# Routing begun two steps earlier, row scatters around GpSimd's products, one group less at the end

## The chip, the cores and the metric

The kernel runs on one core of one Trainium2 chip. The metric is the device time of one launch in microseconds (us), lower is better. A core has five engines that run side by side and wait for each other through semaphores: TensorE (PE in the rows, its weight loads PEld), VectorE (DVE), ScalarE (ACT), GpSimd (POOL) and SyncE (SP), which here only starts transfers. "SPq" is SP's queue of transfers.

## The reference, cut to what matters

The input x is 2 x 2048 tokens of 256 numbers, 4096 tokens in all.

```python
x = layernorm(x + attention(x))     # softmax in windows of 128 tokens, 16 heads, and 64 global tokens
logits = x @ Wg.T                   # 8 experts
top1 = argmax(logits)
xhat = (x - mean) * rsqrt(var + 1e-5)
h = gelu((xhat * ln_scale[top1] + ln_bias[top1]) @ W1[top1] + b1[top1])
out = layernorm(x + h @ W2[top1] + b2[top1])
```

Every token goes through one expert alone, so the kernel sorts the tokens by expert before the expert layers. Softmax runs over all 2048 keys, with scores of zero outside the window and the global pairs; the kernel handles that with sums over the other windows.

## The kernel before, in words

**Attention.** The 4096 tokens are 32 windows of 128. The attention is software-pipelined by steps: in step t each engine works on windows t+2 (queries, keys, values), t (scores and their maximum), t-1 (turned scores, exponentials), t-2 (weighted sums, division), t-3 (output product, residual) and t-4 (layer-norm moments, centring). `step(t, s, steady)` exists once for every engine. Steps 4 to 19 run as a hardware loop of four steps a turn (`LOOP_A = (4, 20)`); the others are written out. Only written-out steps can hold extra work. Step t's row maximum, `row_max_t` (L1181), is the longest VectorE instruction of a step, and its start times mark the steps in a trace: its 31 instructions in the trace belong to steps 1 to 31. Before the maximum of an even step VectorE also subtracts `x_part` (L1012).

**Routing, beside the attention.** `BATCHES` cuts the windows into 0 to 15, 16 to 23 and 24 to 31. For a batch VectorE takes the best expert of each token (`route`), TensorE counts the tokens ahead of each one (`ranks`, at the steps in `RANKS_AT`), VectorE turns these into row numbers (`take_ranks`, `find_places`) and works out the layer-norm factors by Newton steps (`factors`, 15 small instructions). `between_steps(t)` does such work at the end of VectorE's step t, `within_steps(t)` does it behind the queries of the step (L1021, or L1199 where there are none).

**Sorting.** ScalarE scales the centred rows (`SCALED_AT`). GpSimd writes them, 128 rows an instruction, to sorted places in device memory with an indirect transfer (`scatter`, L627). `SCATTERED_AT` gives for a step the windows written at two places of GpSimd's step: ahead of the three small products on guards and logits (L653 to L660), and behind them. Then follow the division `attn_t` (L670), the bias (L675) and the centring (L678). GpSimd's queue is in order, so a scatter holds up what stands behind it. In step 22 GpSimd also clears `w2` (L646).

**Tile list and loads.** `list_tiles` works out, from the first two batches, 16 full tiles of 128 sorted rows (expert and first row of each), and from all three the remaining 24. SP waits for the list and the scatters of the first two batches, loads tiles 0 to 7, then 8 to 15 (L571), writes eight blocks of padding rows (L586), waits for the last batch and the padding, and loads tiles 16 to 39.

**Experts.** Tiles go in pairs 0 to 19. TensorE turns the tiles (L1678), multiplies by the first layer (L1692, L1694), turns the hidden rows (L1701) and multiplies by the second layer (L1710). VectorE adds the residual and takes the moments (`finish`, L1343 to L1352); when a group of `GROUPS` is complete, it works out scale and shift with 13 small dependent instructions (`normalise`). ScalarE applies them (`final`, L840) in pair i+3 or later, up to three tiles a pair, and the rest behind the last pair. GpSimd writes each tile to its tokens' rows of the output (L727). Of the nine tiles behind the last pair VectorE applies four itself (`ON_DVE`: 32, 34, 36, 38), after its last `normalise`; GpSimd writes in tile order.

## Time and profile before

| | us |
|---|---|
| median of 3 runs | 413.27 |
| lowest and highest of them | 410.37, 413.99 |
| the profiled execution, its own time | 411.62 |
| its span in the trace | 409.9 |
| busy: PE, DVE, ACT, POOL | 343.3, 287.7, 224.7, 202.0 |
| scatters of rows (L627), 32 | 31.7 |
| output scatters (L727), 32 of the 40 | 31.6 |
| maxima (L1181), 31 | 70.9 |

The span is what the trace shows from first to last event; the profiled execution took 1.7 us more. Shares of busy time say little here, as the kernel has three stretches with different limits: the attention steps (to about 297 us), the loads and the first expert pairs (to about 345 us), and the remaining pairs and the output (to the end). In a timeline row stand the start, the duration, the engine, the line, what is written and read, how many instructions the row merges, and in brackets how long the engine was idle before and what ended that.

### The profile page before, as it was taken

The numbers are of one execution on the slowest core, as the hardware profiler recorded it, in microseconds if no ns is written. First come the engines' busy times: TensorE is split into PE (matmuls) and PEld (weight loads), VectorE is DVE, ScalarE is ACT, GpSimd is POOL, SyncE is SP. The second block draws the span as 40 slices with busy tenths as digits, with TensorE's granted clock in tenths as the row PEclk, the third lists the DMA queues.
The fourth block names the chain that finished last, engine by engine and source line by source line (L and its number), as shares of the span: only waits on it lengthen the run. The fifth ranks groups of instructions, "written<-read, shape, count | busy, mean of one in ns | idle before, by whom it ended". The sixth has DMA issues, their size and how long they took to land.

```text
span 409.9 us, 12479 instructions
## 1 busy us (share of the span) xinstructions
PE 343.3 (84%) x4437; PEld 283.8 (69%) x4437; DVE 287.7 (70%) x824; ACT 224.7 (55%) x517; POOL 202.0 (49%) x352
## 2 busy tenths in 40 slices
PE   4989899999999999999988999988764797999400
PEld 3858788888888887888777888776442685878200
DVE  7794547667576566675979768797785777779930
ACT  3325576556655765566545788556650444779410
POOL 5243143343533553444443387757584160766763
PEclk9999999999999999999999999999995689999955
DMA  8762571000001000000012011101113463673210
GB/s 237 220 209 85 170 241 42 27 13 15 26 1 26 26 0 26 24 2 27 2 41 66 15 54 45 56 30 43 42 56 96 123 223 106 207 210 101 91 68 0
DMA packets 27976, 31.66 MB, mean 77 GB/s; under 512 B 5184, under 2 KB 25883, under 8 KB 27932
## 3 DMA queue, kind: packets, MB, share of 16 engines
q1 hardware_dynamic: 20246, 18.22, 15.8%
q0 software_dynamic: 3456, 8.66, 5.8%
q10 hardware_dynamic: 4230, 4.22, 3.1%
q8 instruction: 25, 0.41, 0.4%
q14 instruction: 19, 0.15, 0.1%
HBM read 20.96 MB, written 11.17 MB: 78 GB/s over the span
## 4 chain that ended last, share of the span: by engine, by line
PE 46%; DVE 28%; issue 9%; SPq 6%; ACT 5%; POOL 4%; DMA 2%; POOLq 0%; ACTq 0%; DVEq 0%
DVE row_max_t L1181 12%; PE ps L1424 8%; PE ps L1461 8%; PE ps L1386 6%; PE ps L1416 6%; PE ps L1444 4%; PE ps L1438 2%; SPq L570 2%; ACT probs L904 2%; PE ps L1408 2%; DVE other_tiles L1343 2%; SPq L571 2%; PE ps L1428 2%; PE ps L1692 2%; DVE ybn L1348 1%
## 5 line engine op out<-in xcount | busy, mean ns | idle before, releaser
L904 ACT ACTIVATE probs<-ps 128x1024 f32<-128x1024 f32 x64 | 62.1, 1022 | 60.9 <-PE ps L1428 60.8
L1181 DVE TENSOR_REDUCE row_max_t<-ps 128x16 f32<-128x2048 f32 x31 | 70.9, 2287 | 21.2 <-PE ps L1416 21.1
L1424 PE MATMUL ps<-q_slots,k_slots 32*128 32x256 f32 x512 | 40.5, 400 | 9.7 <-DVE row_max_t L1181 8.6
L653 POOL TENSOR_TENSOR bounds_t<-guard_t,bounds_t 128x16 f32<-128x16 f32 x32 | 7.1, 222 | 76.3 <-DVE guard_t L1192 76.3
L670 POOL TENSOR_TENSOR attn_t<-num_t,rden_t 128x256 f32<-128x256 f32 x32 | 19.9, 623 | 48.2 <-DVE rden_t L1210 48.1
L754 ACT ACTIVATE pvT_t<-ps 128x512 f32<-128x512 f32 x34 | 20.3, 598 | 39.9 <-PE ps L1438 37.2
L1416 PE MATMUL ps<-k_slots,q_slots 32*128 32x128 f32 x1056 | 38.7, 283 | 3.2 <-DVE dg L1046 1.3
L1416 PEld LDWEIGHTS ps<-k_slots,q_slots 32*128 32x128 f32 x1056 | 32.5, 186 | 9.2 <-issue 6.4
L727 POOL DMA_INDIRECT out_dram<-other_tiles x32 | 31.6, 988 | 13.8 <-issue 7.0
L627 POOL DMA_INDIRECT sorted_rows<-rows,place_i x32 | 31.7, 991 | 13.3 <-issue 7.8
L915 ACT ACTIVATE boundsT_t<-ps,head_mask 128x128 fp32r<-128x128 f32 x128 | 36.7, 382 | 0.8 <-PE ps L1608 0.7
L1438 PE MATMUL ps<-probs,va 128*32 128x128 f32 x1056 | 35.7, 276 | 0.5 <-ACT boundsT_t L915 0.5
L1386 PE MATMUL ps<-woT,aT_t 128*128 128x264 f32 x128 | 35.9, 405 | 0.0
L1424 PEld LDWEIGHTS ps<-q_slots,k_slots 32*128 32x128 f32 x512 | 20.4, 184 | 17.4 <-DVE row_max_t L1181 16.2
L1408 PE MATMUL ps<-wv_part,x_part 128*128 128x272 f32 x192 | 32.2, 303 | 0.0
L1208 DVE TENSOR_TENSOR num_t<-ps,rest_t 128x272 f32<-128x272 f32 x32 | 14.1, 440 | 24.6 <-PE ps L1444 17.6
L1428 PE MATMUL ps<-boundsT_t,lift 32*128 32x256 f32 x256 | 30.9, 463 | 0.0
L1692 PEld LDWEIGHTS ps<-w1s,xT 128*128 128x128 f32 x160 | 22.6, 205 | 11.0 <-issue 10.6
L1438 PEld LDWEIGHTS ps<-probs,va 128*32 128x32 f32 x1056 | 26.9, 109 | 4.6 <-issue 0.8
L1461 PE MATMUL ps<-x_part,wq_part 128*128 128x256 f32 x192 | 27.0, 290 | 2.2 <-DVE x_part L1012 2.2
L1692 PE MATMUL ps<-w1s,xT 128*128 x160 | 24.7, 297 | 4.1 <-issue 2.9
L1408 PEld LDWEIGHTS ps<-wv_part,x_part 128*128 128x128 f32 x192 | 25.7, 189 | 3.2 <-issue 3.0
(277 smaller groups left out, 798.9 us busy)
## 6 DMA issues: line engine op xcount, KB each, us to landing
table<-rest_sums SPq DMA_DIRECT2D x4, 1088.0 KB, 7.1
other_tiles<-sorted_rows SPq DMA_DIRECT2D x32, 136.0 KB, 2.3
xs<-in_L_attn_x_dram SPq DMA_DIRECT2D x16, 256.0 KB, 2.8
rows<-in_L_attn_x_dram ACTq DMA_DIRECT2D x4, 1024.0 KB, 7.3
sorted_rows<-pad_rows SPq DMA_DIRECT2D x9, 136.0 KB, 2.1
first_tiles<-sorted_rows SPq DMA_DIRECT2D x8, 136.0 KB, 2.2
w<-in_L_ffn_W_dram SPq DMA_DIRECT2D x2, 256.0 KB, 8.0
w<-in_L_ffn_W_dram SPq DMA_DIRECT2D x1, 512.0 KB
```

Source lines behind the costliest of these rows:

```text
L627: pool.indirect_dma_start(sorted_dram[:, :], bass.IndirectOffsetOnAxis(ap=place_i[:, w:w + 1], axis=0), rows[:, w, :], None).then_inc(scat ...
L904: act.activation(probs[:, 2 * h:2 * h + 2, :], ps[:, 2 * h:2 * h + 2, :], ACT.Exp).then_inc(probs_ready, 1)
L915: last = act.activation(boundsT[:, j, :], ps_pv[:, 0:P], ACT.Copy, scale=head_mask[:, j:j + 1])
L1181: dve.tensor_reduce(row_max[:], ps_all, op=ALU.max, axis=AX.X).then_inc(max_ready, 1)
L1386: last = mm(out, lhsT(c), rhs(c), start=(c == 0), stop=(c == KC - 1))
L1408: last = mm(out, rows_part[a][:, c, :], w_part[b][:, c, :], start=(i == 0), stop=(i == len(terms) - 1))
L1416: last = mm(ps[:, u, (2 * c + a) * P:(2 * c + a + 1) * P], q_slots[quad(u), s, c, a, :], k_slots[quad(u), s, c, :], start=True, stop=True, ...
L1424: mm(ps[:, u, 2 * c * P:(2 * c + 2) * P], k_slots[quad(u), s, c, :], q_slots[quad(u), s, c, :, :].rearrange("p a n -> p (a n)"), start=Tru ...
L1428: last = mm(ps[:, u, 2 * c * P:(2 * c + 2) * P], lift[quad(u), :], boundsT[quad(u), 2 * c:2 * c + 2, :].rearrange("p a n -> p (a n)"), sta ...
L1438: last = mm(ps_pv[quad(j), u * P:(u + 1) * P], values[:, h * VP:(h + 1) * VP], weights[:, u, j * P:(j + 1) * P], start=True, stop=True, ti ...
L1461: last = mm(bank[:, o * 2 * P:(o + 1) * 2 * P], w_part[i][b][:, c, o * P:(o + 1) * P], x_part[a][:, c, :, :].rearrange("p w n -> p (w n)") ...
L1692: mm(out, xT[:, i % 2, (2 * k + a) * P:(2 * k + a + 1) * P], w1s[:, k, bass.ds(experts[a], 1), :].rearrange("p e h -> p (e h)"), start=(k ...
```

## The change

It does five things.

1. `LOOP_A` ends at 16: steps 16 to 19 are written out too.
2. The routing of batch 0 starts in step 18 rather than 20, its ranks in 19 rather than 21, its factors in 20 and 21 rather than 21 to 23. Batch 1 starts in step 26 rather than 27 (ranks in 27 rather than 28). The scaled rows follow in steps 22 to 24 rather than 24 to 26.
3. `SCATTERED_AT` has a third place, behind the centring (L678). Three scatters stand in each of steps 23 to 27 and one in 28, where before two or three stood in each of 25 to 30. Of the last eight, steps 32 and 33 before held 4 and 3, all ahead of the division; now step 32 holds 2 ahead and 3 behind its products, and step 33 holds 1.
4. `list_tiles` is split into parts. The list of the first 16 tiles is counted inside step 30 and finished at its end, where it was finished at the end of step 32. For this list the terms that are zero are left out.
5. TensorE's turning of tile pair 0 in step 34 stands behind the last output product rather than ahead of it. In the tail the groups (12, 14) and (14, 16) become (12, 16), so there is one `normalise` less, 13 rather than 9 tiles are applied behind the last pair, and ScalarE applies all of them.

```diff
-        LOOP_A = (4, 20)
+        LOOP_A = (4, 16)
...
-        RANKS_AT = (21, 28, 35)
+        RANKS_AT = (19, 27, 35)
...
-        SCALED_AT = {24: (0, 5), 25: (5, 10), 26: (10, 16), 30: (16, 20), 31: (20, 24)}
-        SCATTERED_AT = {25: (0, 1, 2), 26: (2, 4, 5), 27: (5, 6, 7), 28: (7, 9, 10), 29: (10, 11, 12), 30: (12, 14, 15),
-                        31: (15, 16, 17), 32: (17, 21, 21), 33: (21, 24, 24)}
-        FACTORS_DONE = {24: 1, 30: 2}
+        SCALED_AT = {22: (0, 5), 23: (5, 10), 24: (10, 16), 30: (16, 22), 31: (22, 24)}
+        SCATTERED_AT = {23: (0, 2, 3, 3), 24: (3, 5, 6, 6), 25: (6, 8, 9, 9), 26: (9, 11, 12, 12), 27: (12, 14, 15, 15), 28: (15, 16, 16, 16),
+                        31: (16, 17, 18, 18), 32: (18, 20, 20, 23), 33: (23, 24, 24, 24)}
+        FACTORS_DONE = {22: 1, 30: 2}
...
-        GROUPS = ((0, 4), (4, 8), (8, 12), (12, 14), (14, 16), (16, 18), (18, 20))
+        GROUPS = ((0, 4), (4, 8), (8, 12), (12, 16), (16, 18), (18, 20))
...
+                if not steady and t in SCATTERED_AT:
+                    scatter_rows(*SCATTERED_AT[t][2:4])
...
             for g, t in LAST_FINALS:
-                if t not in ON_DVE:
-                    final(g, t)
+                final(g, t)
...
+                if t == 21:
+                    factors(0, 9, FACTOR_STEPS)
                 if t == 23:
-                    factors(0, 10, FACTOR_STEPS)
-                if t == 25:
                     select_parts()
-                if t == 29:
-                    factors(1, 6, 11)
...
+                if t == 18:
+                    route(0)
+                if t == 19:
+                    find_places(0)
+                if t == 20:
+                    factors(0, 0, 9)
+                if t in (21, 22):
+                    scale_first_layer(t - 21)
+                if t == 26:
+                    route(1)
+                if t == 27:
+                    find_places(1)
+                    factors(1, 0, 2)
+                if t == 28:
+                    factors(1, 2, 11)
+                if t == 29:
+                    jump_tiles(0)
+                if t == 30:
+                    list_tiles(0)
...
-            for t in ON_DVE:
-                dve.tensor_scalar(tile_rows(t, 0, HID), tile_rows(t, 0, HID), yrs[:, t:t + 1], yshift[:, t:t + 1],
-                                  ALU.mult, ALU.add).then_inc(final_dve, 1)
...
-                if not steady and t == PAIRS_FROM:
-                    pe.wait_ge(probs_ready, 2 * NW)
-                    turn_tiles(0)
...
+                if not steady and t == PAIRS_FROM:
+                    pe.wait_ge(probs_ready, 2 * NW)
+                    turn_tiles(0)
                 if not steady and t >= PAIRS_FROM:
                     pair_steps(t - PAIRS_FROM)
```

GpSimd's queue in steps 32 and 33, before (`rest_t` opens a step, `sorted_rows` rows are scatters):

```order
L640 TENSOR_TENSOR rest_t<-table,e_val_t 128x272
L627 DMA sorted_rows<-rows,place_i 33920x272 x4
L670 TENSOR_TENSOR attn_t<-num_t,rden_t 128x256
L675 TENSOR_TENSOR biased_t<-rows,out_bias 128x256
L678 TENSOR_TENSOR rows<-residual_t,mean_var 128x256
L640 TENSOR_TENSOR rest_t<-table,e_val_t 128x272
L627 DMA sorted_rows<-rows,place_i 33920x272 x3
L670 TENSOR_TENSOR attn_t<-num_t,rden_t 128x256
```

and the same place now:

```order
L633 TENSOR_TENSOR rest_t<-table,e_val_t 128x272
L620 DMA sorted_rows<-rows,place_i 33920x272 x2
L663 TENSOR_TENSOR attn_t<-num_t,rden_t 128x256
L668 TENSOR_TENSOR biased_t<-rows,out_bias 128x256
L671 TENSOR_TENSOR rows<-residual_t,mean_var 128x256
L620 DMA sorted_rows<-rows,place_i 33920x272 x3
L633 TENSOR_TENSOR rest_t<-table,e_val_t 128x272
L620 DMA sorted_rows<-rows,place_i 33920x272
L663 TENSOR_TENSOR attn_t<-num_t,rden_t 128x256
```

Seven scatters stood ahead of the last division, four of them ahead of the one before it; now it is six and two.

VectorE's queue at the end of step 21, where GpSimd's clearing of `w2` (the first instruction of GpSimd's step 22 behind `rest_t`) runs beside it, before:

```order
L1241 BN_STATS bn<-residual_t 128x6
L1129 TENSOR_TENSOR place<-place,onehot 128x128
L1130 TENSOR_REDUCE place_f<-place 128x16
L1131 CAST place_i<-place_f 128x16
L1088 TENSOR_SCALAR variances<-stats_t 128x16
L1092 SCALAR_TENSOR_TENSOR variances<-variances,stats_t 128x16
L1012 TENSOR_TENSOR x_part<-ps,x_part 128x512
L1181 TENSOR_REDUCE row_max_t<-ps 128x16
```

and now:

```order
L1248 BN_STATS bn<-residual_t 128x6
L1304 TENSOR_TENSOR w1s<-w,vecT 128x512
L1005 TENSOR_TENSOR x_part<-ps,x_part 128x512
L1188 TENSOR_REDUCE row_max_t<-ps 128x16
L1190 BN_AGGR mean_var<-bn 128x2
```

The three instructions on places have moved to the end of step 19 and the two on variances to step 20; one on the first layer's weights has come from step 24.

## Rows read from the trace of the kernel before

**Rows 1.** The page, the chain of work that ended last, by engine.

```profile
PE 46%; DVE 28%; issue 9%; SPq 6%; ACT 5%; POOL 4%; DMA 2%; POOLq 0%; ACTq 0%; DVEq 0%
```

**Rows 2.** Timeline, VectorE: the maxima of steps 16 to 19.

```profile
161.18 2.29 DVE L1181 TENSOR_REDUCE row_max_t<-ps 128x16 f32<-128x2048 f32 x1
...
169.56 2.29 DVE L1181 TENSOR_REDUCE row_max_t<-ps 128x16 f32<-128x2048 f32 x1 [1.92 <-PE ps L1416]
...
177.49 2.28 DVE L1181 TENSOR_REDUCE row_max_t<-ps 128x16 f32<-128x2048 f32 x1
...
185.69 2.29 DVE L1181 TENSOR_REDUCE row_max_t<-ps 128x16 f32<-128x2048 f32 x1 [1.75 <-PE ps L1416]
```

**Rows 3.** Timeline, VectorE: steps 20 to 23, and GpSimd's clearing of w2.

```profile
193.62 2.28 DVE L1181 TENSOR_REDUCE row_max_t<-ps 128x16 f32<-128x2048 f32 x1
...
202.66 2.28 DVE L1181 TENSOR_REDUCE row_max_t<-ps 128x16 f32<-128x2048 f32 x1
...
210.52 1.85 DVE L1088 TENSOR_SCALAR variances<-stats_t 128x16 f32<-128x16 f32 x1
...
213.10 2.28 DVE L1181 TENSOR_REDUCE row_max_t<-ps 128x16 f32<-128x2048 f32 x1
...
222.75 2.28 DVE L1181 TENSOR_REDUCE row_max_t<-ps 128x16 f32<-128x2048 f32 x1
...
210.51 1.83 POOL L646 MEMSET w<- 128x2048 f32 x1
```

**Rows 4.** Timeline, VectorE: steps 27 to 31.

```profile
255.28 2.29 DVE L1181 TENSOR_REDUCE row_max_t<-ps 128x16 f32<-128x2048 f32 x1 [0.51 <-PE ps L1416]
...
264.20 2.28 DVE L1181 TENSOR_REDUCE row_max_t<-ps 128x16 f32<-128x2048 f32 x1
...
273.98 2.28 DVE L1181 TENSOR_REDUCE row_max_t<-ps 128x16 f32<-128x2048 f32 x1
...
290.79 2.29 DVE L1181 TENSOR_REDUCE row_max_t<-ps 128x16 f32<-128x2048 f32 x1
```

**Rows 5.** Timeline, GpSimd in step 25, one scatter ahead of the guards.

```profile
240.08 1.19 POOL L627 DMA_INDIRECT sorted_rows<-rows,place_i  x1 [0.18 <-issue]
241.63 0.21 POOL L653 TENSOR_TENSOR bounds_t<-guard_t,bounds_t 128x16 f32<-128x16 f32 x1 [0.37 <-DVE guard_t L1192]
...
244.28 0.62 POOL L670 TENSOR_TENSOR attn_t<-num_t,rden_t 128x256 f32<-128x256 f32 x1 [0.81 <-DVE rden_t L1210]
```

**Rows 6.** Timeline and chain, steps 32 and 33: scatters, reciprocal, division, the last scatter's landing.

```profile
298.75 1.01 POOL L627 DMA_INDIRECT sorted_rows<-rows,place_i  x1 [0.16 <-issue]
...
301.28 0.25 DVE L1210 RECIPROCAL rden_t<-num_t 128x16 f32<-128x16 f32 x1
...
303.59 0.63 POOL L670 TENSOR_TENSOR attn_t<-num_t,rden_t 128x256 f32<-128x256 f32 x1
...
308.91 2.44 DMA sorted_rows<-rows,place_i
```

**Rows 7.** Timeline, SP's queue and TensorE's wait: tiles 0 to 7, 8 to 15, padding, tiles from 16 on.

```profile
312.50 8.53 SPq L571 DMA_DIRECT2D first_tiles<-sorted_rows  x8
321.93 8.00 SPq L571 DMA_DIRECT2D other_tiles<-sorted_rows  x8
330.73 9.13 SPq L586 DMA_DIRECT2D sorted_rows<-pad_rows  x8
...
345.66 0.66 PE L1678 MATMUL ps<-ident,other_tiles 128*128 128x128 f32 x4 [2.29 <-DMA other_tiles<-sorted_rows]
```

**Rows 8.** Timeline, the output: GpSimd's scatters of tiles 16 and 32; ScalarE, VectorE.

```profile
371.34 0.99 POOL L727 DMA_INDIRECT out_dram<-other_tiles  x1 [1.43 <-ACT other_tiles L840]
...
393.60 1.03 POOL L727 DMA_INDIRECT out_dram<-other_tiles  x1 [1.91 <-ACT other_tiles L840]
...
380.50 1.58 ACT L840 ACTIVATE other_tiles<-other_tiles,yshift,yrs 128x256 f32<-128x256 f32 x3
...
392.39 1.38 DVE L1375 TENSOR_SCALAR other_tiles<-other_tiles,yrs,yshift 128x256 f32<-128x256 f32 x4
```

More of the change, by code:

```diff
@@ L488, in windowed_attention_then_top1_experts @@
         FINALS, LAST_FINALS = final_places()
-        ON_DVE = tuple(t for k, (g, t) in enumerate(LAST_FINALS) if k % 2 == 1)
-        def finals_before(t):
-            order = [x[1] for part in FINALS for x in part] + [x[1] for x in LAST_FINALS]
-            ahead = order[:order.index(t) + 1]
-            return (final_dve, sum(x in ON_DVE for x in ahead)) if t in ON_DVE else (final_act, sum(x not in ON_DVE for x in ahead))
+        FINAL_ORDER = [t for part in FINALS for g, t in part] + [t for g, t in LAST_FINALS]
         @block.sync
@@ L1131, in find_places, with count_tiles, jump_tiles @@
                 dve.tensor_copy(place_i[:, part], place_f[:, part]).then_inc(places_ready, 1)
[L1133 to L1143 removed]
+            own_ends, ends = sums[:, 0, EXPERTS:], [sums[:, i, EXPERTS:] for i in range(4)]
+            def count_tiles(part):
+                link(dve.tensor_tensor(tiles_of[:], base[:, LISTED_AFTER[part], :], base[:, 0, :], ALU.subtract))
+                link(dve.tensor_scalar(count_i[:, 0, :], tiles_of[:], P - 1.0 if part else 0.0, None, ALU.add))
+                link(dve.tensor_scalar(count_i[:, 1, :], count_i[:, 0, :], 7, None, ALU.logical_shift_right))
+                if part:
                     link(dve.tensor_copy(tiles_of[:], count_i[:, 1, :]))
                     link(dve.tensor_tensor(own_ends, tiles_of[:], done[:, 0:EXPERTS], ALU.subtract))
+                else:
+                    link(dve.tensor_copy(own_ends, count_i[:, 1, :]))
+            def jump_tiles(part):
+                if part:
                     link(dve.tensor_scalar(jump[:], own_ends, -float(P), float(SEG), ALU.mult, ALU.add))
@@ L1160, in list_tiles, with mark_tiles @@
                 dve.tensor_scalar(tile_row[:, first:first + k], start_at[:, 0, 0:k], float(DUMMY), None, ALU.min).then_inc(lists_ready, 1)
-                if not last_part:
-                    link(dve.tensor_tensor(tiles_of[:], own_ends, ends[3], ALU.subtract))
-                    link(dve.tensor_scalar(tiles_of[:], tiles_of[:], float(k), 0.0, ALU.add, ALU.max))
-                    link(dve.tensor_tensor(tiles_of[:], tiles_of[:], own_ends, ALU.min))
-                    link(dve.tensor_tensor(done[:, 0:EXPERTS], done[:, 0:EXPERTS], tiles_of[:], ALU.add))
+            def mark_tiles(part):
+                link(dve.tensor_tensor(tiles_of[:], own_ends, ends[3], ALU.subtract))
+                link(dve.tensor_scalar(tiles_of[:], tiles_of[:], float(TILES[part]), 0.0, ALU.add, ALU.max))
+                link(dve.tensor_tensor(done[:, 0:EXPERTS], tiles_of[:], own_ends, ALU.min))
             def step(t, s, steady=False):
@@ L1289, in between_steps @@
                     factors(2, 0, FACTOR_STEPS)
-                    list_tiles(1, 0)
+                    count_tiles(1)
+                    jump_tiles(1)
+                    sum_tiles(1)
             def scale_first_layer(k):
@@ L1368, in _ @@
                 if i == 0:
-                    list_tiles(1, 1)
+                    list_tiles(1)
                 for g, (a, b) in enumerate(GROUPS):
```

51 lines of the change are left out of this document (15 added, 36 removed).

## The prediction

> **What bounds the kernel now.** I read the chain of waits first [rows 1]: TensorE and VectorE hold 74% of it, and no engine holds it alone. So a moved instruction is worth what its place is worth, and I cut the run by what ends each stretch.
>
> To about 297 us the steps end it. In an undisturbed pair of steps the maxima of steps 17, 18 and 19 start 7.93 and 8.20 us apart [rows 2]; odd steps take the first, even ones the second. The maximum of an odd step starts after VectorE has been idle for 1.75 to 1.92 us [rows 2]: that is the room for extra VectorE work at the end of an even step. Work beyond it lengthens the step. The step ahead of the loop's turn, 16, took 8.38 [rows 2], 0.18 over an even step. Steps 20, 21 and 22, with the routing of batch 0, took 9.04, 10.44 and 9.65 [rows 3], 29.13 against 24.33 for the same three undisturbed (8.20 + 7.93 + 8.20): 4.80 too long. Steps 27 and 28 took 8.92 and 9.78, and 29 and 30 together 16.81 [rows 4].
>
> From step 32 GpSimd is the late engine: the division of step 32 was ready to start at 301.53, when the reciprocal ended, and started at 303.59, right behind four scatters [rows 6]. The last scatter of the first two batches landed at 311.35 [rows 6]. From there SP's queue runs without a gap that another engine makes: two sets of eight loads, eight paddings, then tiles 16 on [rows 7], and TensorE, idle for 2.29 us, starts the second set of pairs at 345.66 when the first of these tiles is there [rows 7]. Whatever moves the last early scatter moves that point by as much, while TensorE's own pairs stay within these 2.29 us.
>
> At the end GpSimd's output scatters follow each other every 1.29 us (31.6 us for 32 of them is 0.99 each, with 0.30 between). The run that starts with tile 16 at 371.34 would reach tile 32 at 371.34 + 16 x 1.29 = 391.98, but tile 32 starts at 393.60 after 1.91 idle [rows 8]. Tile 32 is one of those that VectorE applies after all its other work, at 392.39 [rows 8].
>
> **The change, part by part.**
>
> Batch 0's routing. Step 18 gets what step 20 had, at the same kind of place: 9.04. Step 19 gets the places of step 21, but not the variances. These began 7.86 us into step 21 (210.52 - 202.66) [rows 3]; there the subtraction of `x_part` and then the maximum can follow, 0.6 later (the variances' 1.85, a short follower of 0.1 and this 0.6 make up the 2.58 to 213.10 [rows 3]). So step 19 takes 8.46. Step 20 gets nine of the factor instructions where step 22 had eight and took 9.65 [rows 3]; one more, at the tail where they are short, adds 0.2: 9.88. Together 27.38 against 24.33 undisturbed: 3.05 too long, where it was 4.80. **Gain 1.75.** The six factor instructions inside step 21 stand where five stood in step 23, in VectorE's idle time ahead of the sums; if that were full, one more would cost 0.2.
>
> Nearly all of this comes from one row. The variances, an instruction on 128x16 numbers, took 1.85 us, from 210.52 to the end of GpSimd's clearing of `w2` (210.51, 1.83 long) [rows 3]. Clearing stays in step 22, and now the weight product of 128x512 and the maximum run beside it. The question is whether they wait as well. The maxima took 2.28 or 2.29 in every step shown, whatever GpSimd did [rows 2, 3, 4], so I let them pass. The weight product starts some 1.5 us ahead of the clearing, which begins 7.85 into the step (210.51 - 202.66) [rows 3], and should be done by then. If it did wait, it would give back up to the 1.68 that 1.85 is over a short 0.17. The Trainium skill, SBUF — State Buffer, section "Who interferes with whom", says that a VectorE instruction with two SBUF inputs competes with GpSimd only where GpSimd reads SBUF, while a `tensor_scalar` can enter the two-port mode and wait. By it the scaling never waits for a clearing and the gain is whole; by a lock on every VectorE instruction the gain would shrink to 0.1. The row shows only the `tensor_scalar` half of that.
>
> Batch 1's routing. In step 27 it took 8.92 [rows 4], of which 0.6 was the subtraction of `x_part` behind it. In step 26 no subtraction follows: 8.3 to 8.5, say 8.4, 0.2 over an even step. Step 27 now has ranks, places and two variance instructions at its end: like 19, but on half the numbers, 8.9. Step 28 gets nine factor instructions behind its end, as step 20 does: 9.85 against 9.78 before [rows 4]. Step 29 holds little, 7.93. Step 30 had eight small instructions at its end and now has seven bigger ones there and eight inside: 8.9 to 9.1, say 9.0, where before it was 16.81 - 7.93 = 8.88 [rows 4]. Sum for 26 to 30: 44.1 against 8.2 + 35.51 = 43.7 [rows 4]. **Loss 0.4**, 0 to 1.0.
>
> The loop. One turn less saves the 0.18 of step 16 and about 0.1 ahead of it: **gain 0.3**. If fetching the new code cost anything, steps 20 to 23, the first behind the loop now, would have shown it; step 23 is of the plain length.
>
> Scatters beside the steps. Step 25 had one scatter ahead of the guards, 1.3 us with its gap, and the guards then waited 0.37 for VectorE; the division waited 0.81 [rows 5]. Steps 23, 25 and 27 now have two there. The guards come about 0.9 later, which nobody waits for, and the division slips from 0.81 early to just in time, since 0.37 and 0.81 together are nearly one scatter. I cost it at nothing. The cover is gone: a scatter of 1.4 instead of 1.3 would show in each odd step. ScalarE's five scaled rows in the odd step 23 cost what they cost in step 25. The list's new place only makes it early; the scatters, not the list, release the loads.
>
> Steps 32 and 33. From 298.75 on two scatters end at 301.3, the division starts behind the reciprocal at 301.7 (instead of 303.59 [rows 6]), with bias and centring it ends 2.0 later, three scatters take 3.85 with the gap, the product that opens step 33 takes 0.7 with its gap, and the last scatter starts at 308.1 to 308.2, instead of 308.91 [rows 6]. **Gain 0.8** (above: one whole scatter, 1.27; below: 0.3 if a product is slower). The earlier output product brings the last batch forward by about 2 us, which is slack already: SP is still at the paddings. It counts only in keeping TensorE and the last scatters out of the way.
>
> The tail. GpSimd's run from tile 16 no longer stops at 32, if ScalarE has the new group of eight (24 to 31) in time. Tile 24 is due at 371.34 + 8 x 1.29 = 381.7; ScalarE applied three tiles from 380.50 on, 28 to 30, whose group also ended with pair 15 [rows 8]; 24 to 26 now stand in that place, and VectorE is there no later, having one `normalise` less ahead of it. The first is applied at 381.0. Tile 36 is due at 397.1, and its values were there before 392.39 [rows 8]. So tile 32 starts at 391.98 instead of 393.60: **gain 1.6** (0 if the group comes over 2 us later than that, 1.9, the whole idle time, at most). The four tiles that VectorE no longer applies cost ScalarE 2 us, beside GpSimd's run.
>
> Sum: 1.75 - 0.4 + 0.3 + 0.8 + 1.6 = 4.05, say 4.1. The profiled execution would go from 411.62 to 407.5. Its time is 1.65 under the median of the three runs; the four executions average 412.3. From that 408.2, from the median 409.2; I take **408.7**.
>
> **Rivals.**
>
> *The clearing finds another victim*, the weight product or the maximum. For: 1.85 for a tiny instruction [rows 3] shows that the wait is real. Against: the constant maxima. Then the gain is 4.1 - 1.7 = 2.4: 410.9 from the median.
>
> *The tail keeps its gap*, because the group of eight comes late for tile 24, or ScalarE with 13 tiles behind the last pair does. For: only 0.7 us of room at tile 24. Against: each later tile has more. Gain 2.5: 410.8.
>
> *GpSimd becomes the bound of steps 23 to 27*, slower than before. Three scatters a step are 3.9 us beside products that leave an odd step no room [rows 5]. Where a third scatter fits nowhere, each of the five steps grows by up to its 1.29 us, 6.4 in all, and the kernel ends at 411.62 - 4.1 + 6.4 = 413.9, by the median 415.6. It decides from 0.8 us a step on. Against: of the 0.37 and 0.81 idle little is missing [rows 5], and even steps have room for two scatters ahead of the guards already before the change. A scatter took 1.19 once in step 25 rather than 0.99 to 1.01 [rows 5, 6]. The Trainium skill's same page, section "SBUF: two separate sides", has VectorE's two-port instructions lock GpSimd out of writing a transfer's descriptors; it would make this rival worse, while 31.7 us for 32 scatters shows little of it.
>
> *The loads do not follow*: the last batch's scatters or TensorE's pairs then end the wait at 345.66, so only part of the 2.45 us gained upstream arrives. Against: the last batch itself comes earlier. Gain 3: 410.3.
>
> **Chances.** The forecast as it stands 0.55; the clearing 0.12; the tail 0.12; GpSimd 0.08; the loads 0.08; something larger than the forecast (the contended instructions find free places) 0.05. A difference of about 1%, 4.1 us, is what a measurement of this kernel tells from none, and the forecast lies right on it. So about half of the forecast's cases, most of its upper side and the 0.05 are faster by over 1%: faster 0.45. Within 1%: the rest of it, the partial rivals and half of GpSimd's: 0.49. Slower: 0.06. The range: the forecast's own bounds (upstream 0.5 to 2.3, scatters 0.3 to 1.3, tail 0.8 to 1.9) give a gain of 1.6 to 5.5, and the runs differ by 3.6 among themselves. From 405.2 to 412.0.
>
> **What the profile of the changed kernel would show.** No VectorE instruction of small size that lasts 1.8 us; the maxima of steps 18 to 21 at 9.0, 8.5 and 9.9 us from each other, and those of 21 to 26 at the undisturbed 7.9 and 8.2 (23 a little more); `attn_t` of step 32 right behind its reciprocal; the last early scatter 2.5 us earlier than before, and the first pair on tile 16 with it, still after a wait for the load; 24 output scatters without a gap from tile 16 to 39. I would be wrong if odd steps 23, 25 and 27 exceed 8.3 us with `attn_t` right behind a scatter, if the first pair on tile 16 is not released by its load, or if GpSimd idles ahead of tile 24 or 32.

## The result

| | before | after |
|---|---|---|
| median of 10 runs each, us | 411.30 | 408.84 |
| lowest and highest, us | 410.37, 413.99 | 406.66, 410.46 |
| profiled execution, us | 411.62 | 409.35 |
| its span, us | 409.9 | 407.6 |
| busy: PE, DVE, ACT, POOL, us | 343.3, 287.7, 224.7, 202.0 | 347.4, 281.1, 226.3, 201.6 |

The ratio is 0.9921, with a 95% interval of 0.9892 to 0.9950: about 0.8% faster, under the 1% that the prediction took as its bound. The forecast, 408.7, is 0.14 from the median. That flatters it. It was 4.1 under 412.8, a base between the average of four executions (412.3) and the median of the first three (413.27), and over more runs the kernel before is at 411.3 to 411.6. The gain of the profiled execution is 2.27, where the sum said 4.1.

### The profile page after: what moved, and what is told of

Same layout as the page of the kernel before. It is cut to its first block, busy times and chain, and to the rows that moved or that the text cites. A ratio compares the mean times of both kernels' runs of the same rounds, so it can differ in the third digit from the quotient of the medians.

```text
span 407.6 us, 12386 instructions
## 1 busy us (share of the span) xinstructions
PE 347.4 (85%) x4437; PEld 287.8 (71%) x4437; DVE 281.1 (69%) x803; ACT 226.3 (56%) x521; POOL 201.6 (49%) x352
## 4 chain that ended last, share of the span: by engine, by line
PE 52%; DVE 22%; issue 8%; SPq 6%; ACT 5%; POOL 3%; DMA 2%; POOLq 0%; DVEq 0%; ACTq 0%
DVE row_max_t L1188 11%; PE ps L1430 9%; PE ps L1467 8%; PE ps L1392 6%; PE ps L1422 6%; PE ps L1450 4%; PE ps L1444 3%; PE ps L1698 3%; PE ps L1716 2%; PE ps L1414 2%; SPq L563 2%; POOL out_dram L721 2%; ACT probs L898 2%; PE ps L1434 2%; SPq L564 2%
## 5 line engine op out<-in xcount | busy, mean ns | idle before, releaser
L1698 PEld LDWEIGHTS ps<-w1s,xT 128*128 128x128 f32 x160 | 25.0, 225 | 10.5 <-issue 10.3
L1698 PE MATMUL ps<-w1s,xT 128*128 x160 | 27.4, 319 | 3.5 <-ACT xT L748 2.0
```

The lines of the kernel that those rows point to most:

```text
L1698: mm(out, xT[:, i % 2, (2 * k + a) * P:(2 * k + a + 1) * P], w1s[:, k, bass.ds(experts[a], 1), :].rearrange("p e h -> p (e h)"), start=(k ...
```

## The profile after

The page, the row of the granted clock (40 slices of 10.2 us) and the chain of work by engine.

```profile
PEclk9999999999999999999999999998997579999955
PE 52%; DVE 22%; issue 8%; SPq 6%; ACT 5%; POOL 3%; DMA 2%; POOLq 0%; DVEq 0%; ACTq 0%
```

VectorE lost six points of the chain and TensorE gained six [rows 1]. The 8 in the slice at 275 us is new.

Timeline, VectorE, the maxima of steps 18 to 22 and 26 to 31 (columns as in [rows 2]).

```profile
177.43 2.28 DVE L1188 TENSOR_REDUCE row_max_t<-ps 128x16 f32<-128x2048 f32 x1
186.47 2.28 DVE L1188 TENSOR_REDUCE row_max_t<-ps 128x16 f32<-128x2048 f32 x1
194.96 2.29 DVE L1188 TENSOR_REDUCE row_max_t<-ps 128x16 f32<-128x2048 f32 x1
204.90 2.28 DVE L1188 TENSOR_REDUCE row_max_t<-ps 128x16 f32<-128x2048 f32 x1
212.82 2.28 DVE L1188 TENSOR_REDUCE row_max_t<-ps 128x16 f32<-128x2048 f32 x1
...
245.34 2.28 DVE L1188 TENSOR_REDUCE row_max_t<-ps 128x16 f32<-128x2048 f32 x1
254.24 2.28 DVE L1188 TENSOR_REDUCE row_max_t<-ps 128x16 f32<-128x2048 f32 x1
262.92 2.27 DVE L1188 TENSOR_REDUCE row_max_t<-ps 128x16 f32<-128x2048 f32 x1
272.68 2.28 DVE L1188 TENSOR_REDUCE row_max_t<-ps 128x16 f32<-128x2048 f32 x1
281.84 2.29 DVE L1188 TENSOR_REDUCE row_max_t<-ps 128x16 f32<-128x2048 f32 x1 [1.75 <-PE ps L1422]
290.12 2.28 DVE L1188 TENSOR_REDUCE row_max_t<-ps 128x16 f32<-128x2048 f32 x1
```

Steps 18, 19 and 20 took 9.04, 8.49 and 9.94 (forecast 9.04, 8.46, 9.88), and 21 took 7.92. Steps 27 and 28 took 8.68 and 9.76 (8.9, 9.85), but step 26 took 8.90 (8.4), step 29 took 9.16 (7.93) and step 30 only 8.28 (9.0).

Timeline, VectorE and then GpSimd, the end of step 21.

```profile
211.07 0.99 DVE L1304 TENSOR_TENSOR w1s<-w,vecT 128x512 f32<-128x512 f32 x1
...
212.82 2.28 DVE L1188 TENSOR_REDUCE row_max_t<-ps 128x16 f32<-128x2048 f32 x1
...
213.08 1.81 POOL L639 MEMSET w<- 128x2048 f32 x1
```

The clearing runs beside the maximum, which keeps its 2.28. It found no new victim [rows 3].

Step 29: TensorE's timeline around its wait for the maximum, then two stretches of 4 us (busy time and count of PE, PEld, DVE, ACT and POOL, the granted clock, DMA's share, GB/s).

```profile
275.02 0.71 PE L1430 MATMUL ps<-q_slots,k_slots 32*128 32x256 f32 x8 [2.08 <-DVE row_max_t L1188]
...
276.98 1.97 PE L1392 MATMUL ps<-woT,aT_t 128*128 128x264 f32 x4
...
278.81 1.57 PE L1414 MATMUL ps<-wv_part,x_part 128*128 128x272 f32 x6
```

```profile
272.00:276.00 4.00, 1.92 (x30) 1.67 (x30) 3.75 (x13) 1.10 (x3) 0.56 (x3) 1.00 0.02 4
276.00:280.00 4.00, 4.00 (x26) 3.25 (x19) 1.75 (x7) 2.68 (x5) 1.82 (x3) 0.58 0.00 0
```

Behind 2.08 us of waiting the clock went to its lower level (1.2 instead of 2.4 GHz; 0.58 is the mean of the stretch). The output product took 1.97, where it takes 1.06 at full clock, and the values product 1.57, where it takes 0.99. VectorE waited for the first. In the kernel before the same wait was 1.77 long, and 275 to 283 had a clock of 1.00.

Steps 32 and 33, the loads and TensorE's wait for tile 16: GpSimd's timeline, SP's queue, TensorE's timeline.

```profile
301.02 0.61 POOL L663 TENSOR_TENSOR attn_t<-num_t,rden_t 128x256 f32<-128x256 f32 x1 [0.69 <-DVE rden_t L1217]
...
307.43 1.01 POOL L620 DMA_INDIRECT sorted_rows<-rows,place_i  x1 [0.17 <-issue]
```

```profile
311.08 8.52 SPq L564 DMA_DIRECT2D first_tiles<-sorted_rows  x8
...
341.01 18.29 SPq L564 DMA_DIRECT2D other_tiles<-sorted_rows  x16
```

```profile
344.27 0.66 PE L1684 MATMUL ps<-ident,other_tiles 128*128 128x128 f32 x4 [1.67 <-DMA other_tiles<-sorted_rows]
344.77 1.75 PE L1716 MATMUL ps<-w,hT 128*128 x4
...
348.44 0.60 PE L1684 MATMUL ps<-ident,other_tiles 128*128 128x128 f32 x4
```

From the maximum of step 31 to the last early scatter it is 17.31 (307.43 - 290.12), before 18.12 (308.91 - 290.79) [rows 4, 6]. The loads follow: tile 16 is 1.39 earlier at TensorE [rows 7]. Behind this wait the clock fell as well. A product of 1.03 took 1.75, and from its turning of the tiles to that of the next pair the pair took 4.17 (348.44 - 344.27), before 3.13 (348.79 - 345.66).

The output, GpSimd's scatters of tile 16 and of the last tile; every one of the 23 that follow tile 16 starts 0.30 behind the one ahead.

```profile
370.76 0.98 POOL L721 DMA_INDIRECT out_dram<-other_tiles  x1 [1.48 <-ACT other_tiles L834]
...
400.42 0.98 POOL L721 DMA_INDIRECT out_dram<-other_tiles  x1 [0.30 <-issue]
```

Tile 16 leaves only 0.58 earlier than before (371.34 [rows 8]); of the 1.39 at TensorE, 0.8 is gone. From tile 16 to the last one it is 29.66, before 31.34 (402.68 - 371.34): 1.68 won.

## The experiments

All were timed against the kernel before, whose median was 411.5 to 411.6 beside them. The changed kernel was timed in another session, so between it and its variants the ratios are the better measure, and both are given where they differ. My theory: every term was about right, and what is missing from 4.1 are falls of TensorE's clock behind waits, of which the forecast had none. The rivals: the total of VectorE's work decides, wherever it stands; GpSimd is the bound; the gains don't add.

**The tail alone**, on the kernel before.

```diff
-        GROUPS = ((0, 4), (4, 8), (8, 12), (12, 14), (14, 16), (16, 18), (18, 20))
+        GROUPS = ((0, 4), (4, 8), (8, 12), (12, 16), (16, 18), (18, 20))
-        ON_DVE = tuple(t for k, (g, t) in enumerate(LAST_FINALS) if k % 2 == 1)
+        ON_DVE = ()
```

> The kernel before with the tail of the change alone: pairs 12 to 15 as one group, and ScalarE applies all tiles. Theory (the forecast's tail term): GpSimd's output scatters run from tile 16 to 39 without a gap, 1.29 us apart; tile 32 no longer waits for VectorE; 1.6 us faster than before, ratio 0.996. Rival (the tail keeps its gap): the group of eight comes late for tile 24 or ScalarE is late with 13 tiles, the gap of 1.9 us moves, and the time stays within 0.3 us of before.

409.72, ratio 0.9960 [0.9947, 0.9974]: by the ratio 1.6 of the 1.6 forecast. In its profile the output runs from tile 16 (370.61) to the last one (400.27) in the same 29.66.

**The clearing alone**, on the kernel before.

```diff
-                if not steady and t == WEIGHTS_AT:
+                if not steady and t == WEIGHTS_AT - 2:
```

> The kernel before with GpSimd's clearing of w2 in step 20 instead of 22, nothing else. Theory (the port is what costs): at the end of step 21 the variances take 0.2 to 0.5 us instead of 1.85, step 21 takes 8.7 to 9.1 instead of 10.44, and beside the clearing, now at the end of step 19, the subtraction and the maximum keep 0.69 and 2.28; 1.4 to 1.7 us faster than before, ratio 0.996 to 0.997. Rival: the variances are slow for another reason, or another VectorE instruction takes the wait: no more than 0.3 us.

409.95, ratio 0.9958 [0.9942, 0.9973]: 1.7. VectorE's timeline at the end of step 21:

```profile
210.90 0.16 DVE L1088 TENSOR_SCALAR variances<-stats_t 128x16 f32<-128x16 f32 x1
```

The instruction that took 1.85 [rows 3] takes 0.16, and step 21 takes 8.76 instead of 10.44. The clearing now runs from 193.82 to 195.63, beside the subtraction and the maximum of step 20, and they keep their 0.69 and 2.28. Steps 18 to 25 take 67.87 in this profile, where the whole rearrangement brings them to 67.91: what batch 0 gained is the place of the clearing, and starting its routing earlier brought nothing of its own.

**Turns in step 29.** A turn here is a transpose of the identity whose result nobody reads. The changed kernel, with eight ahead of TensorE's wait for the maximum:

```diff
+                if not steady and t == 29:
+                    pe.wait_ge(qf_ready, NW // 2)
+                    for r in range(8):
+                        nc.tensor.transpose(ps_xq[:, (r % 4) * P:(r % 4 + 1) * P], ident[:], ident[:])
                 if prev:
                     pe.wait_ge(max_ready, upto(t + 1))
```

> The changed kernel with eight more 128x128 turns of the unit matrix into a free bank (about 1.3 us of TensorE) in step 29, ahead of TensorE's wait for the maximum; they add work and compute nothing that is used. In the changed kernel's trace TensorE idled 2.08 us there, its granted clock then halved, and step 29 took 9.16 us instead of 7.93. Clock theory: without most of that idle time the clock stays full, step 29 takes 7.9 to 8.2, and the kernel is 1.0 to 1.3 us faster than the changed one (by the profile 406.4 in place of 407.6), if no other place falls. Rival (step 29 is long by its dependences, or the clock falls for another reason): step 29 stays over 8.8 and the time is the changed kernel's or up to 0.5 us more.

407.37, ratio 0.9911 [0.9878, 0.9943]. TensorE's timeline, and the stretch behind:

```profile
272.08 1.04 PE L1582 MATMUL ps<-ident 128*128 128x128 f32 x8
274.32 0.71 PE L1430 MATMUL ps<-q_slots,k_slots 32*128 32x256 f32 x8 [1.21 <-DVE row_max_t L1188]
...
276.13 1.06 PE L1392 MATMUL ps<-woT,aT_t 128*128 128x264 f32 x4
```

```profile
275.00:279.00 4.00, 3.98 (x57) 3.21 (x53) 2.38 (x9) 3.19 (x8) 2.02 (x5) 1.00 0.01 2
```

The wait ends as it did, but 1.21 of it is idle instead of 2.08, the clock stays, and the step takes 7.71 instead of 9.16. The interval of the times overlaps that of the changed kernel, and one trace without a fall doesn't show that the turns prevented it. It shows what a fall costs: 1.45. Whether turns hold the clock is decided further down.

**Turns ahead of tile 16**, six, in the changed kernel.

```diff
                 j = i - TILES[0] // 2
+                if j == 0:
+                    need(pe, tileT_ready, i - 1)
+                    for r in range(6):
+                        nc.tensor.transpose(ps[:, i % 2, (r % 4) * P:(r % 4 + 1) * P], ident[:], ident[:])
```

> The changed kernel with six more 128x128 turns of the unit matrix (about 1 us of TensorE) ahead of the wait for the load of tile 16; they are overwritten. In the changed kernel's trace the clock was halved for some 3 us behind this wait, and the next pair took 5.54 us instead of 4.66. Clock theory: the clock stays full there, and the point where GpSimd starts on tile 16 comes 0.8 us earlier than in the changed kernel, ratio 0.998 against it. Rival: the clock falls there anyway or TensorE is not what paces the pairs, and the time is unchanged.

407.94, ratio 0.9911 [0.9889, 0.9933]. TensorE's timeline:

```profile
341.00 0.82 PE L1683 MATMUL ps<-ident 128*128 128x128 f32 x6
343.97 0.66 PE L1688 MATMUL ps<-ident,other_tiles 128*128 128x128 f32 x4 [2.15 <-DMA other_tiles<-sorted_rows]
344.46 1.03 PE L1720 MATMUL ps<-w,hT 128*128 x4
...
347.13 0.60 PE L1688 MATMUL ps<-ident,other_tiles 128*128 128x128 f32 x4
```

From turning to turning 3.16 instead of 4.17. What is still idle, 2.15, is more than the 1.67 behind which the clock fell without the turns. So the length of the last wait alone does not decide.

**The earlier output product undone.**

```diff
+                if not steady and t == PAIRS_FROM:
+                    pe.wait_ge(probs_ready, 2 * NW)
+                    turn_tiles(0)
                 if pp:
                     pe.wait_ge(probs_ready, 2 * (t - 1))
...
-                if not steady and t == PAIRS_FROM:
-                    pe.wait_ge(probs_ready, 2 * NW)
-                    turn_tiles(0)
```

> The changed kernel, but TensorE turns tile pair 0 ahead of the last output product again, as before. Forecast (the product's early place is slack only): TensorE waits for the first tile load until 314.5 and does the product for window 31 behind it, at about 315.5 instead of 310.19; the last batch's eight row scatters end at about 336 to 337, still 3 us before SP has done the paddings (338.1); SP's load of tiles 16 on starts at 341.0 as now, the time is the changed kernel's 408.8 within 0.3. A detail of the clock: TensorE is idle in one long piece of 4 us rather than in 3.7 and 2.7, and has no product in the middle; pairs 0 to 7 start from the same halved clock. Rival (the early place is what makes the last batch in time): the load of tiles 16 on starts later than 341.0 by what the batch is late, 1 us or more, and the time is 409.8 or more.

407.94, ratio 0.9925 [0.9897, 0.9952], by the ratio the same as the changed kernel. The product started at 314.96, the last batch's scatters ended at 336.06, and the tiles from 16 on were loaded from 340.71: slack, as forecast. The trace showed more than was asked. The steps to 31 are the changed kernel's, instruction for instruction, yet here the clock fell in step 21 and not in 29. TensorE's timeline in step 21, and stretches of steps 21 and 29:

```profile
206.89 1.01 PE L1430 MATMUL ps<-q_slots,k_slots 32*128 32x256 f32 x8 [1.73 <-DVE row_max_t L1188]
...
210.03 1.33 PE L1392 MATMUL ps<-woT,aT_t 128*128 128x264 f32 x4
```

```profile
207.00:211.00 4.00, 4.00 (x32) 3.23 (x33) 1.98 (x11) 1.72 (x2) 0.60 (x3) 0.57 0.05 18
...
277.00:281.00 4.00, 3.98 (x57) 3.22 (x53) 2.18 (x7) 3.46 (x8) 2.02 (x5) 1.00 0.01 2
```

Step 21 took 9.29 instead of 7.92 and step 29 took 7.72 instead of 9.16. So the same code falls in one execution and not in another: the wait says where it can happen, not whether. With the changed routing, nothing spread and no turns ahead of them, the wait of step 29 (2.08 to 2.10 idle) was followed by a fall in four of five profiles and that of step 21 (1.73 or 1.74) in one of six; in the kernel before and its three variants without turns step 29 waits 1.57 to 1.77 and never fell. Without turns, the wait for tile 16 showed it in four of six profiles with the changed routing (idle 1.41 to 1.70 where it fell, 1.52 and 2.29 where it did not), and in none of the four of the kernel before and its variants (2.29 and 2.23 idle in two).

**All five scatters of step 32 ahead of the products.**

```diff
-                        31: (16, 17, 18, 18), 32: (18, 20, 20, 23), 33: (23, 24, 24, 24)}
+                        31: (16, 17, 18, 18), 32: (18, 23, 23, 23), 33: (23, 24, 24, 24)}
```

> The changed kernel, but all five scatters of step 32 stand ahead of its three GpSimd products instead of two ahead and three behind; one stays in step 33. Theory (the 0.8 us gained in steps 32 and 33 comes of six scatters there instead of seven, and of no idle time): the five run from 298.1 to 304.2 without a gap, the division of step 32 starts at 304.3 instead of 301.02, GpSimd loses the 0.69 idle ahead of it, and the last early scatter starts at 306.7 to 307.4 (now 307.43). TensorE's turning of the divided window comes 3.3 later, and with it the division of step 33 (now 308.48) at 308.5 to 311; that is absorbed by the slack of the last batch. Time 408.1 to 408.9. Rival (the order around the products is what gains): the last early scatter starts at 308.2 or later, SP's loads and the first pair on tile 16 move with it, the time is 409.6 or more.

407.51, ratio 0.9902 [0.9878, 0.9926], under the 408.1 to 408.9 that I expected. The last early scatter started at 306.98, 16.72 behind the maximum of step 31 instead of 17.31. So the 0.8 came of six scatters instead of seven; by these two profiles, standing around the products cost 0.6 of what that brings.

**The factor work spread.** In the changed kernel step 20 keeps 4 instructions instead of 9, step 28 has 3 instead of 9; the rest stands in steps 21 and 29, the scaling of the weights in 22 and 24.

```diff
-                    factors(0, 9, FACTOR_STEPS)
+                    factors(0, 4, 10)
...
-                    factors(1, 11, FACTOR_STEPS)
+                    factors(1, 5, 11)
...
-                    factors(0, 0, 9)
-                if t in (21, 22):
-                    scale_first_layer(t - 21)
+                    factors(0, 0, 4)
+                if t == 21:
+                    factors(0, 10, FACTOR_STEPS)
+                if t in (22, 24):
+                    scale_first_layer(t // 2 - 11)
...
-                    factors(1, 2, 11)
+                    factors(1, 2, 5)
...
+                    factors(1, 11, FACTOR_STEPS)
```

> The changed kernel, but the factor work is spread: batch 0 has 4 of its 15 instructions at the end of step 20, 6 within and 5 at the end of 21 (instead of 9 and 6), the scaling of the first layer's weights stands in steps 22 and 24 (instead of 21 and 22), batch 1 has 2 at the end of 27, 3 at the end of 28, 6 within and 4 at the end of 29 (instead of 2, 9, 4). Theory (what exceeds VectorE's 1.8 us of room at a step's end lengthens the step and idles TensorE; behind a long enough idle the granted clock falls): step 20 at 8.9 to 9.2 instead of 9.94, step 21 at 8.0 to 8.3 instead of 7.92 (five small ones fit into an odd step's end only in part), step 28 at 8.7 to 9.0 instead of 9.76, step 29 at 8.2 to 8.5 instead of 9.16 with a granted clock of 1.00 from 276 to 280. Sum gained 2.0 to 2.9 us; time 405.9 to 406.8. Rival (the total of VectorE's work counts, wherever it stands): the four steps sum to the same 36.8, the time stays 408.8.

405.83, ratio 0.9870 [0.9840, 0.9899]: 3.0 under the changed kernel by the medians, 2.1 by the ratios. Steps 20, 21, 28 and 29 took 8.81, 8.77, 8.20 and 8.01, 33.79 instead of 36.78. Of these 2.99, 1.45 is the fall in step 29, which this profile doesn't have; against the 35.33 without it the spread alone is worth 1.54. The total of the work is the same, so the rival (the total decides) falls all the same. I had step 21 too short and 28 too long. For step 21 the timelines of VectorE and then GpSimd show why:

```profile
209.90 0.49 DVE L1065 SCALAR_TENSOR_TENSOR newton_t<-ln_factor 128x32 f32<-128x32 f32 x1
210.43 0.54 DVE L1067 TENSOR_TENSOR newton_t<-newton_t,variances 128x32 f32<-128x32 f32 x1
211.00 0.57 DVE L1068 SCALAR_TENSOR_TENSOR ln_factor<-newton_t,ln_factor 128x32 f32<-128x32 f32 x1
211.60 0.18 DVE L1089 TENSOR_TENSOR newton_t<-variances,ln_factor 128x16 f32<-128x16 f32 x1
...
211.46 1.80 POOL L639 MEMSET w<- 128x2048 f32 x1
```

The first three, at a place where GpSimd has its products of 128x256, cost three times the 0.18 to 0.20 that such instructions take elsewhere. The fourth runs beside the clearing of `w2` and takes its plain 0.18.

**Spread, and turns ahead of tile 16.** Both edits as above.

> The spread factors and, ahead of TensorE's wait for tile 16, six turns of a constant block whose result nobody reads. If the two clock falls are independent of each other, the gains add: 2.0 to 2.9 of the spread and 0.9 of the turns (which alone made 407.94 of the changed kernel's 408.8): 405.0 to 406.0, the pair on tile 16 then 3.1 to 3.2 us from its first turn to the next pair's first turn. Rival (TensorE's pairs are not what bounds the end, GpSimd's output run is, and it starts with its values): the turns bring nothing more, the time is that of the spread alone.

405.45, ratio 0.9866 [0.9834, 0.9898], the fastest kernel here. Whether the turns add to the spread stays open: the two differ by 0.4, and the one without turns had no fall in its profile.

**Turns at all four long waits**, in the changed kernel and in the kernel before (for that one `t in (23, 29, 30)`).

```diff
+                if not steady and t in (21, 29, 30):
+                    pe.wait_ge(aT_ready, t - 2)
+                    for r in range(8):
+                        nc.tensor.transpose(ps_rao[:, HID + (r % 2) * P:HID + (r % 2 + 1) * P], ident[:], ident[:])
                 if prev:
                     pe.wait_ge(max_ready, upto(t + 1))
...
+                if j == 0:
+                    need(pe, tileT_ready, i - 1)
+                    for r in range(6):
+                        nc.tensor.transpose(ps[:, i % 2, (r % 4) * P:(r % 4 + 1) * P], ident[:], ident[:])
```

> The changed kernel with turns of a constant block, whose result nobody reads, in TensorE's three longest waits for the maximum (8 each in steps 21, 29 and 30, idle there 1.73, 2.08 and 1.47 us) and ahead of its wait for tile 16 (6). Theory (falls of the granted clock behind such waits, now at one place, now at another, are what the forecast left out): no stretch of the steps from 16 to 31 at a clock under 1.00, 127.3 from the maximum of step 16 to that of 31 instead of 128.80 (290.12 - 161.32), and 406.0 to 406.9 instead of 408.8; against the kernel before with the same turns it is 4.0 to 4.7 faster, which is what my terms summed to. Rival (the falls cost the kernel before as much as the changed one): the turned kernels differ by the same 2.5 to 3.0 as the plain ones.

> The kernel before with the same turns in its three longest waits for the maximum (steps 23, 29 and 30, idle 1.54, 1.77 and 1.68 us) and ahead of its wait for tile 16. Its profiled execution shows no fall at these places (277 to 280 at full clock), so by the theory the turns bring it little: 410.7 to 411.4, with the executions above 413 gone. By the rival it gains as much as the changed kernel does, and is at 408.9 to 409.5.

The changed kernel with turns: 406.06, ratio 0.9873 [0.9856, 0.9889], its five runs between 405.95 and 407.09, where without turns ten lay between 406.66 and 410.46. The kernel before with turns: 411.71, ratio 1.0004 [0.9981, 1.0026]. So the rival falls. The falls cost the changed kernel 2.8 by the medians and 2.0 by the ratios, whose intervals just miss each other, and the kernel before nothing that can be measured. In the changed kernel with turns the stretches of 275 to 279 and 342 to 347 have a clock of 1.00, and from the maximum of step 16 to that of 31 it takes 127.36 (127.3 expected). The clock of whole executions says the same, and it doesn't hang on one profile: their mean granted clock was 0.934 to 0.946 in the ten of the changed kernel and 0.946 to 0.950 in the five with turns; in the kernel before it was 0.933 to 0.953 without and 0.930 to 0.953 with turns. The turns themselves cost the steps of the kernel before nothing: from the maximum of step 16 to that of 31 it takes 129.60 with them, 129.61 without.

Two of my numbers were off. The kernel before came out above the 410.7 to 411.4 that I expected and kept its spread (410.64 to 416.01), so that has another cause, which stays open; its slowest execution had the lowest clock of the twelve, 0.930, but no trace was taken of it. And the turned kernels are 5.6 apart, more than the 4.7 I allowed. From load to output the profiles differ by 1.7 that no term of mine names (0.85 from SP's first load to that of tile 16, 0.85 from there to the output of tile 16), and the gap at tile 32 was 2.42 in that profile instead of 1.91.

**A fourth scatter in an odd step**, in the changed kernel.

```diff
-        SCATTERED_AT = {23: (0, 2, 3, 3), 24: (3, 5, 6, 6), 25: (6, 8, 9, 9), 26: (9, 11, 12, 12), 27: (12, 14, 15, 15), 28: (15, 16, 16, 16),
+        SCATTERED_AT = {23: (0, 2, 3, 3), 24: (3, 5, 5, 5), 25: (5, 8, 9, 9), 26: (9, 11, 12, 12), 27: (12, 14, 15, 15), 28: (15, 16, 16, 16),
```

> The changed kernel with one row scatter moved from step 24 to the odd step 25, which then has three ahead of the guards and one behind, four in all. It tests the price that the prediction put on a bound by GpSimd. Theory (the division waits only for what stands ahead of it; now it waits 0.54 for VectorE): four scatters from 238.2 end the guards at 242.6 to 242.7 and the division starts at 243.7 to 243.9 instead of 242.73, right behind a scatter; TensorE's turning of the divided window and the work behind it come 1.1 later, and step 25 takes 8.6 to 9.1 instead of 7.93. Rival (the division has slack of its own on TensorE's side): step 25 stays at 7.9 to 8.2.

409.14 (two runs), step 25 took 8.50 instead of 7.93. GpSimd's timeline:

```profile
241.94 0.99 POOL L620 DMA_INDIRECT sorted_rows<-rows,place_i  x1 [0.17 <-issue]
242.96 0.63 POOL L663 TENSOR_TENSOR attn_t<-num_t,rden_t 128x256 f32<-128x256 f32 x1
```

The division stands right behind a scatter, 6.08 behind the maximum of its step (242.96 - 236.88) instead of 5.32 (242.73 - 237.41). A scatter's 1.27 less the 0.54 that was idle is 0.73, not my 1.0 to 1.2. GpSimd does become the bound here, at the fourth scatter; with three, step 25 has 0.54 left and step 27 0.72. Step 23 has nothing left: there the first scatter took 1.19, and the division started right behind the third, at 226.43, 0.18 after its reciprocal had ended.

**Two edits together**, the clearing in step 20 and the tail, on the kernel before.

```diff
-                if not steady and t == WEIGHTS_AT:
+                if not steady and t == WEIGHTS_AT - 2:
...
-        GROUPS = ((0, 4), (4, 8), (8, 12), (12, 14), (14, 16), (16, 18), (18, 20))
+        GROUPS = ((0, 4), (4, 8), (8, 12), (12, 16), (16, 18), (18, 20))
-        ON_DVE = tuple(t for k, (g, t) in enumerate(LAST_FINALS) if k % 2 == 1)
+        ON_DVE = ()
```

> The kernel before with only two edits: the clearing of w2 in step 20 instead of 22, and the new groups and values of the tail. Each alone gave a ratio of 0.996. Theory (one is upstream of the loads, the other behind them, and they add): 408.1 to 408.4, ratio 0.991 to 0.993, no slower than the whole change with its routing two steps earlier. Rival (the gain of the moved clearing reaches only TensorE's wait for tile 16 and the tail's gap hides the rest): 409.3 or more.

408.63, ratio 0.9930 [0.9905, 0.9955], a little over the 408.1 to 408.4 expected. They nearly add (by the ratios 2.9 of 3.4), and do what the whole change does (408.84).

## Why the prediction was right or wrong, step by step

- **Batch 0: right.** Forecast 1.75. Steps 18 to 25 took 69.59 before and 67.91 after: 1.68. The clearing alone brings 1.7, and the same in these steps.
- **The loop: right.** Step 16 took 8.18 instead of 8.38, step 15 took 7.93 instead of 8.02: 0.29 of the 0.3.
- **Batch 1: the step that failed.** Forecast a loss of 0.4; steps 26 to 30 took 43.71 before and 44.78 after, a loss of 1.07. The sentence that failed is "Step 29 holds little, 7.93": it measured 9.16. It looked only at what VectorE does there, not at what TensorE's wait ahead of it, 0.3 longer than before, can bring. With turns at the waits the five steps take 43.34, a gain of 0.37: without the fall the term was too pessimistic, since step 30 kept to 8.28 although it has more to do.
- **Scatters in the odd steps: right, with less cover than it sounds.** Step 25 took 7.93 with two ahead of the guards, and its division waited 0.54 for VectorE. Step 23 took 8.22, where step 25 had taken 8.22 before, both with a first scatter of 1.19 and the selection of the bias rows; which of the two makes it 0.3 long stays open. In step 23 the division already waited for the scatter, for 0.18. The rival with GpSimd as the bound begins there, and costs a step 0.57 at the fourth scatter.
- **Steps 32 and 33: right in size** (0.81 of 0.8), by luck in part: the number of scatters brought it, and their places gave 0.6 back.
- **The loads follow: right**, 1.39 at TensorE. But the forecast let this arrive at the output whole. Behind a wait that the row of before already showed [rows 7] the clock fell, the pair took 1.0 longer, and 0.58 arrived. From the turning of tile 16 to its output it is 26.49 here and was 25.68 before. In the four profiles with a fall there it is 25.80 to 26.49, in the ten others 25.16 to 25.97, on average 0.7 less.
- **The tail: right**, 1.68 of 1.6; 1.6 alone. The narrow place is the one that the prediction named, tile 24: in four of the variants' profiles GpSimd waited there for ScalarE, 0.41 to 0.83 instead of 0.30.

Against the 4.1, then: -1.45 for the fall in step 29, some -0.8 behind tile 16, +0.8 for batch 1 without its fall, and -0.4 for the rest make the 2.27 of the profiled execution. Of that rest 0.24 lies ahead of step 17, whose maximum starts at 169.50, only 0.06 earlier [rows 2]: the loop's gain is real in its steps, but the maximum of step 16 starts anywhere from 160.53 to 161.55 in the 14 profiles, and this pair happened to differ the wrong way. That the time came out at the forecast is luck: a base 1.5 too high (412.8 instead of 411.3) stood beside a gain 1.6 too large (4.1 instead of 2.46). The range held it, and of the chances "within 1%", where it is, had the most, 0.49.

The rule of the Trainium skill, SBUF — State Buffer, section "Who interferes with whom", held: the weight product and the maximum were not lengthened. The weight product does not test it, since it ended at 212.06 and the clearing began at 213.08. The spread kernel does: there a product with two inputs in SBUF (`newton_t`, 211.60) ran inside the clearing (211.46 to 213.26) and took its 0.18, while the `tensor_scalar` of the kernel before took 1.85 beside it. In the other spread profile it is the same (0.18 at 210.93, the clearing from 210.78). So a lock on every VectorE instruction is ruled out.

## What to carry to other kernels

A moved instruction costs what its place costs, on both sides: two edits, one that moves a clearing and one that drops a small group, bring here what the whole rearrangement brings. When a change lengthens a wait of TensorE, or only leaves one of 1.5 to 2 us in place, add a term for its clock, read the granted clock in the windows behind each such wait, and compare several executions, because one profile shows one draw. A few products that nobody reads, put into the wait, are a cheap test and here also a remedy.

## What the runs showed of the hardware that I had not expected

- The clock falls behind waits of 1.4 to 2.1 us, in some executions and not in others, and costs 1.4 where VectorE waits for the product behind it, 1.0 in a pair. Across places the length of the wait does not order the cases: 1.41 fell, 2.29 did not. At one place it goes with them: in step 29, 2.1 us fell in four of five profiles, 1.57 to 1.77 in none of four. What decides stays open.
- The small instructions of the routing wait for GpSimd far more often than the one row on the clearing tells. In step 22 of the kernel before, the timelines of VectorE and then GpSimd:

```profile
219.26 0.49 DVE L1067 TENSOR_SCALAR newton_t<-variances 128x32 int32<-128x32 int32 x1
219.79 0.54 DVE L1069 TENSOR_SCALAR ln_factor<-newton_t 128x32 int32<-128x32 int32 x1
220.36 0.58 DVE L1072 SCALAR_TENSOR_TENSOR newton_t<-ln_factor 128x32 f32<-128x32 f32 x1
220.97 0.95 DVE L1074 TENSOR_TENSOR newton_t<-newton_t,variances 128x32 f32<-128x32 f32 x1
221.95 0.19 DVE L1075 SCALAR_TENSOR_TENSOR ln_factor<-newton_t,ln_factor 128x32 f32<-128x32 f32 x1
...
218.98 0.74 POOL L675 TENSOR_TENSOR biased_t<-rows,out_bias 128x256 f32<-128x256 f32 x1
219.67 0.61 POOL L678 TENSOR_TENSOR rows<-residual_t,mean_var 128x256 f32<-128x256 f32 x1
220.25 0.65 POOL L640 TENSOR_TENSOR rest_t<-table,e_val_t 128x272 f32<-128x272 f32 x1
220.84 1.04 POOL L617 COPY q_slots<-qf 128x1024 f32<-128x1024 f32 x1
```

The last stands alone and takes 0.19; the four ahead of it run while GpSimd does its products and its copy of 128x1024 (220.84 to 221.88), and take 2.56 together, 1.8 more than four times 0.19. Each of the four ends 0.03 to 0.05 behind the end of one GpSimd instruction (219.72, 220.28, 220.90, 221.88). It is so everywhere: between 190 and 300 us the 14 profiles have 148 products and `tensor_scalar` instructions of VectorE on at most 128x32 numbers that take over 0.3, and every one ends within 0.1 of the end of a GpSimd instruction. Held they are; that it is GpSimd's reads that hold the products, and not any work of it, rests on the few that passed beside the clearing in the two spread profiles. No run here took GpSimd's products away.
